# Starting the large arrays of a shared SBUF buffer on 64-byte lines

## The chip, the cores and the metric

The kernel runs on one core of a Trainium2 chip. The metric is the device time of one execution in microseconds, as the median of three runs.

## What is computed

The input `x` is four sequences of 1024 rows with 256 features. Four residual layers follow one another, each on the normalised rows:

```python
x = x + attn_a(layernorm(x))    # complex linear recurrence over time, dense layers, gelu, layernorm
x = x + ffn(layernorm(x))      # top-32 gating of outputs and inputs per row, 256x256 product
x = x + attn_b(layernorm(x))   # softmax attention, 8 heads of 64, keys and values through a rank of 64
x = x + ffn(layernorm(x))      # the same gated layer, same weights
```

The recurrence is an `associative_scan` with a complex factor per feature; its real and imaginary parts go through two 256x256 products, and two more dense layers follow. The gated layer takes a softmax of 256 logits per row, keeps the 32 largest (once to gate the outputs, once the inputs) and multiplies by one weight matrix:

```python
s_v_out, s_i_out = top_k(softmax(bottleneck_out(x)), 32)
out_branch = scatter(take(x @ weight, s_i_out) * s_v_out)
s_v_in, s_i_in = top_k(softmax(bottleneck_in(x)), 32)
in_branch = scatter(take(x, s_i_in) * s_v_in) @ weight
return out_branch + in_branch + bias
```

## The kernel before

The 4096 rows lie on 128 partitions as 32 tiles of 128 rows; eight chunks of four tiles make the units of the first layer. The program has four stages. The recurrence stage works chunk by chunk: TensorE projects the normalised rows (L1675, L1703), VectorE turns and scans them (L1334 to L1368), TensorE multiplies the states `h` (L1716) and the two dense layers (L1731 on `outT`, L1743 to L1749 on `y1T`). A gated layer works tile by tile: VectorE finds the 32 largest of 256 logits twice with eight MAX8 (L1487) and eight MATCH_REPLACE8 (L1492), ScalarE takes exponentials and moves PSUM results out (`zfT` at L983, `sxT` at L1028, `gs` at L1016, `fs` at L1023), GpSimd does seven elementwise steps of 128x256 (L743 to L762). The attention stage works through 64 items (batch, head, half of the rows); for each, TensorE computes the scores twice (L1966 with queries as weights for the row maxima, L1978 and L1980 with keys as weights) and the weighted sum (L1995 to L1997, 96 small matmuls with the exponentials `pr_hi` and `pr_lo` as weights and `lat` as the moving operand); ScalarE takes the exponentials (L1140) and rounds them to fp16 (L1148), and GpSimd and VectorE form the remainders (L819, L1592). The last stage is the gated layer again.

The order of the instructions on each engine is written out by hand; semaphores alone tie the engines together. Memory in SBUF is of two kinds. Some tensors are allocated by themselves (`x`, `zrow`, `zT`, `xcT`, `ident`, `fW`, `lin`, the transformed attention weights `qkA`, `voB` and others). Everything else is cut from one tensor, `arena`, of 27,800 four-byte words per partition, by a counter:

```python
        def carve(shape, dt=F32, parts=P):
            ...
            words = n if dt == F32 else (n + 1) // 2
            a = arena[0:parts, room[0]:room[0] + words]
            room[0] += words
```

The counter is set back to reuse the room in later stages: `room[0] = 0` before the gated layer's arrays, `room[0] = after_rows` before those of attention, `room[0] = after_setup` for the weights that are only transformed once. No array is padded, so a small array (`norm`, `obias`, `nm`, `sm` have two words each) shifts everything carved after it. In the built program `arena` itself begins at byte 96,992 of a partition, which is 32 bytes past a multiple of 64; of the separate tensors `x`, `xcT`, `ident`, `ident16` and `minus_ident16` begin on a multiple of 64, and `zrow`, `zT`, `fW`, `fbias`, `lin`, `qkA`, `voB` 32 bytes past one.

Of the kernel before, what the change touches and what calls it, by code (L numbers as in the profile page):

```python
# [37 lines left out]
GROUP = 4  # L38
GROUPS = NH // 2
Q_RING = 4  # L40
Z_RING = 4
AHEAD = 2

# [4 lines left out]
def hybrid_block_kernel(nc, x_in, W_in, b_in, params_log, W_mid, b_mid, w1_w, w1_b, w2_w, w2_b,  # L48
# [4 lines left out]
    with ctx:  # L53
# [51 lines left out]
        arena = sb("arena", [P, ARENA])  # L105
        room = [0]

        def carve(shape, dt=F32, parts=P):
            n = 1
            for s in shape:  # L110
                n *= s
            words = n if dt == F32 else (n + 1) // 2
            a = arena[0:parts, room[0]:room[0] + words]
            room[0] += words
            assert room[0] <= ARENA, room[0]
            if dt != F32:
                a = a.bitcast(dt)
            if len(shape) == 2:
                a = a.rearrange("p (a b) -> p a b", a=shape[0])
            if len(shape) == 3:  # L120
                a = a.rearrange("p (a b c) -> p a b c", a=shape[0], b=shape[1])
            return a


        cosT = carve([KB2, CH])
        win = carve([3, KB2, D])
        wmid = carve([2, KB2, D])
        w1 = carve([KB2, D])
        w2 = carve([KB2, D])
# [12 lines left out]
        gam = carve([D])  # L142
        sinT = carve([KB2, CH])
        decT = carve([KB2, CH])
        front_at = room[0]
        turned = [[carve([KB2, CH]) for _ in range(2)] for _ in range(2)]
        pa, pb = carve([KB2, CH]), carve([KB2, CH])
        ta, tb = carve([KB2, CH]), carve([KB2, CH])
# [15 lines left out]

        zf = [carve([D]) for _ in range(Z_RING)]
        zfT = [carve([KB2, P]) for _ in range(2)]
# [16 lines left out]
        after_ffn = room[0]  # L183
# [4 lines left out]
        pr_hi = [carve([TIME // P, CH], F16) for _ in range(2)]  # L188
        pr_lo = [carve([TIME // P, CH], F16) for _ in range(2)]

        room[0] = max(room[0], after_ffn)
        qA = carve([Q_RING, TIME], F16)
        qB_words = arena[:, room[0]:room[0] + Q_RING * TIME // 2]
        qB = carve([Q_RING, TIME], F16)
        kB_words = arena[:, room[0]:room[0] + TIME]
# [248 lines left out]
        def place(W):  # L444

            B, w = W // ITEMS, W % ITEMS
            hh, c = w // 2, w % 2
            return B, hh, c, hh % Q_RING

# [23 lines left out]
        def wait_from(engine, sem_, value):  # L473

            if value > 0:
                engine.wait_ge(sem_, value)
# [41 lines left out]
        def _(sp):  # L518
# [26 lines left out]
            def load(head):  # L545

                B, hh, slot = head // NH, head % NH, head % Q_RING
                if head % NH == 0:
                    for k in (2 * B, 2 * B + 1):
                        sp.wait_ge(s_qst[k], 2 * GROUPS * 16)  # L550
                wait_from(sp, s_qld, head * 48)
                wait_from(sp, a_sps, (head - Q_RING + 1) * 2 * KT)
                for half in range(2):
# [30 lines left out]
        def _(pool):  # L584
# [154 lines left out]
            def tail(f, t, p):  # L739
# [6 lines left out]
                pool.wait_ge(f_z, T + 1)  # L746
                nc.gpsimd.tensor_tensor(sx[p], dd[p][:, 1, :], zf[t % Z_RING], ALU.mult).then_inc(f_s, 1)
                pool.wait_ge(f_er, T * 2 + 2 + CREDIT["f_er"])
# [103 lines left out]
        def _(act):  # L852
# [118 lines left out]
            def z_tile(t, dst):  # L971
                return nc.scalar.activation(dst.unsqueeze(1), x[:, bass.ds(t, 1), :], ACT.Identity,
                                            bias=rs[:, bass.ds(t, 1), 1], scale=rs[:, bass.ds(t, 1), 0])

            def ffn_z(f, t):
                T = t + f * NT
                wait_from(act, f_s, T - Z_RING + 1)
                z_tile(t, zf[t % Z_RING]).then_inc(f_z, 1)

# [243 lines left out]
        def _(dve):  # L1223
# [413 lines left out]
            def last_tile(f, t, p):  # L1637
# [5 lines left out]
                dve.wait_ge(f_d_last, 1)  # L1643
                nc.vector.tensor_tensor(sx[p], dd[p][:, 1, :], zf[t % Z_RING], ALU.mult).then_inc(f_s, 1)
                dve.wait_ge(f_gps, T + 1)
# [10 lines left out]
        def _(pe):  # L1656
# [150 lines left out]
            def ffn_z_turned(f, t, p):  # L1807
                T = t + f * NT
                pe.wait_ge(f_z, T + 1)
                if not (isinstance(T, int) and T == 0):  # L1810
                    pe.wait_ge(f_zT, T + 0)
                z = zf[t % Z_RING]
                for k in range(KB2):
# [313 lines left out]
```

## Time and profile before

| | |
|---|---|
| median of three runs | 1379.68 us (1375.58 to 1380.49) |
| the profiled execution, its own time | 1381.49 us |
| its span in the trace | 1379.8 us |
| busy over the span | PE 88%, DVE 83%, ACT 76%, POOL 70% |
| mean granted TensorE clock | 0.968 of full speed |

"Busy" is the time in which an engine has an instruction in work. A matmul's duration in the trace includes its way through the array, so consecutive matmuls overlap; the distance from one start to the next tells their rate. The stages lie in the trace about at 0 to 260 us (recurrence), 260 to 505 us (first gated layer, with the projections of the first attention batches beside it), 505 to 1150 us (attention) and 1150 to 1380 us (second gated layer).

### The profile page before, as it was taken

What the parts mean: (1) busy time and instruction counts of PE and PEld (TensorE: products, weight loads), DVE (VectorE), ACT (ScalarE), POOL (GpSimd) and SP (SyncE); (2) the same over time, 40 slices, a digit from 0 to 9 for tenths busy, and PEclk for the clock granted to TensorE, in tenths of its full rate; (3) what the DMA queues carried; (4) which work ended last, traced back from release to release, by engine and by line L of the source; (5) the groups of instructions that cost most, each with busy time, mean ns of one, the idle gap of its engine ahead of it and who ended that gap; (6) DMA issues with size and microseconds to landing.
All of it is one profiled execution on the core that took longest, in us unless ns stands there. A gap on an engine that the chain in (4) does not pass through costs nothing.

```text
span 1379.8 us, 30641 instructions
## 1 busy us (share of the span) xinstructions
PE 1218.1 (88%) x10192; PEld 743.8 (54%) x10192; DVE 1149.0 (83%) x3141; ACT 1054.9 (76%) x2350; POOL 963.6 (70%) x1094
## 2 busy tenths in 40 slices
PE   3999999767888879999999999999999999667776
PEld 1455554334455536665666666666666666344444
DVE  6999998479998888888777787878777854799998
ACT  3432333677899869999999989999999985777775
POOL 4457644368777767778777778777777773488887
PEclk9999999989999999999999999999999999899997
DMA  6200000000012000000000000000000000000000
GB/s 174 77 1 1 0 1 0 1 1 1 12 36 77 31 17 25 25 25 25 25 13 14 2 2 2 2 3 2 2 2 2 2 2 1 1 31 17 31 17 31
DMA packets 35529, 25.32 MB, mean 18 GB/s; under 512 B 16358, under 2 KB 32044, under 8 KB 35372
## 3 DMA queue, kind: packets, MB, share of 16 engines
q1 hardware_dynamic: 35372, 23.36, 6.0%
q8 instruction: 82, 1.34, 0.4%
q14 instruction: 75, 0.61, 0.1%
HBM read 14.89 MB, written 8.39 MB: 17 GB/s over the span
## 4 chain that ended last, share of the span: by engine, by line
PE 57%; DVE 13%; issue 13%; ACT 12%; POOL 4%; DVEq 0%; DMA 0%; SPq 0%; ACTq 0%; POOLq 0%
PE banks L1978 7%; PE banks L1980 6%; PE banks L1966 6%; DVE arena L1492 4%; PE banks L1716 4%; PE banks L1924 4%; PE banks L1995 4%; PE banks L1996 4%; PE banks L1997 3%; DVE arena L1487 3%; ACT arena L1140 3%; PE banks L1675 3%; ACT arena L1148 2%; PE banks L1731 2%; PE banks L1900 2%
## 5 line engine op out<-in xcount | busy, mean ns | idle before, releaser
L819 POOL TENSOR_TENSOR arena<-arena 128x512 f16<-128x512 f32 x383 | 438.0, 1163 | 150.1 <-ACT arena L1148 146.4
L1140 ACT ACTIVATE arena<-banks 128x512 f32<-128x512 f32 x512 | 303.1, 600 | 45.1 <-PE banks L1980 40.3
L1566 DVE TENSOR_REDUCE arena<-banks 128x1 f32<-128x512 f32 x512 | 325.5, 679 | 5.1 <-PE banks L1966 2.8
L1148 ACT ACTIVATE arena<-arena 128x512 f16<-128x512 f32 x512 | 315.9, 632 | 0.0
L1487 DVE MAX8 arena<-arena 128x8 f32<-128x256 f32 x512 | 190.6, 414 | 27.4 <-issue 15.9
L1995 PE MATMUL banks<-arena 128*128 128x65 f16 x2016 | 211.3, 193 | 1.1
L1996 PE MATMUL banks<-arena 128*128 128x64 f16 x2016 | 211.4, 195 | 0.0
L1997 PE MATMUL banks<-arena 128*128 128x65 f16 x2016 | 210.5, 192 | 0.0
L1592 DVE TENSOR_TENSOR arena<-arena 128x512 f16<-128x512 f32 x129 | 106.8, 828 | 123.6 <-ACT arena L1148 123.5
L1492 DVE MATCH_REPLACE8 arena<-arena 128x256 f32<-128x256 f32 x512 | 206.0, 410 | 0.4 <-issue 0.2
L1995 PEld LDWEIGHTS banks<-arena 128*128 128x128 f16 x2016 | 187.9, 96 | 32.0 <-issue 10.1
L1996 PEld LDWEIGHTS banks<-arena 128*128 128x128 f16 x2016 | 187.3, 97 | 27.1
L1978 PE MATMUL banks<-arena 128*128 128x512 f16 x512 | 194.1, 379 | 8.2 <-ACT arena L1140 6.8
L1966 PE MATMUL banks<-arena 128*128 128x512 f16 x512 | 194.5, 382 | 4.6 <-DVE arena L1566 4.6
L1980 PE MATMUL banks<-arena 128*128 128x512 f16 x512 | 193.8, 378 | 0.0
L1997 PEld LDWEIGHTS banks<-arena 128*128 128x128 f16 x2016 | 187.4, 99 | 0.0
L1847 PE MATMUL banks<-fW,arena 128*128 128x256 f32 x256 | 80.5, 441 | 32.2 <-ACT arena L1028 32.2
L1966 PEld LDWEIGHTS banks<-arena 128*128 128x128 f16 x512 | 57.9, 113 | 74.5 <-DVE arena L1566 16.2
L1978 PEld LDWEIGHTS banks<-arena 128*128 128x128 f16 x512 | 50.3, 98 | 48.9 <-ACT arena L1140 31.5
L1834 PE MATMUL banks<-fW,arena 128*128 128x256 f32 x256 | 76.6, 428 | 0.0
L1826 PE MATMUL banks<-lin,xcT 128*128 128x512 f32 x128 | 71.5, 641 | 5.0 <-ACT xcT L1032 5.0
L1847 PEld LDWEIGHTS banks<-fW,arena 128*128 128x128 f32 x256 | 46.9, 203 | 52.1 <-ACT arena L1028 47.9
(223 smaller groups left out, 2543.3 us busy)
## 6 DMA issues: line engine op xcount, KB each, us to landing
arena<-q_store SPq DMA_DIRECT2D x48, 128.0 KB, 2.7
x<-in_L_attn_a_x SPq DMA_DIRECT2D x8, 512.0 KB, 3.9
q_store<-arena SPq DMA_DIRECT2D x32, 128.0 KB, 1.8
out<-x SPq DMA_DIRECT2D x7, 512.0 KB, 2.9
arena<-arena SPq DMA_DIRECT2D x64, 1.0 KB, 1.9
arena<-in_L_attn_a_W_in SPq DMA_DIRECT2D x1, 768.0 KB, 5.7
arena<-in_L_attn_a_W_mid SPq DMA_DIRECT2D x1, 512.0 KB, 7.5
arena<-in_L_attn_a_w_w SPq DMA_DIRECT2D x2, 256.0 KB, 7.8
```

What stands on the lines that cost most here:

```text
L819: nc.gpsimd.tensor_tensor(pr_lo[c][:, kt, :], pr[:, kt, :], pr_hi[c][:, kt, :], ALU.subtract).then_inc(a_lP, 1)
L1140: nc.scalar.activation(pr[:, kt, :], ps[6 + kt % 2][:, :], ACT.Exp, scale=SM_SCALE).then_inc(a_P, 1)
L1148: nc.scalar.activation(pr_hi[c][:, kt, :], pr[:, kt, :], ACT.Copy).then_inc(a_hi, 1)
L1487: nc.vector.max(m8[p][:, i, r, :], src).then_inc(f_k[i], 1)
L1492: nc.vector.match_replace(wk[p][:, i, r % 2, :], m8[p][:, i, r, :], src, TAKEN).then_inc(f_k[i], 1)
L1566: nc.vector.tensor_reduce(mx_half[c][:, i // 2, i % 2:i % 2 + 1], ps[n % MAX_BANKS][:, :], X, ALU.max).then_inc(a_mx, 1)
L1966: mm(ps[n % MAX_BANKS][:, :], every[:, j, :], kA[B % 2][:, half * CH:half * CH + CH], start=True, stop=True).then_inc(a_mps, 1)
L1978: mm(o[:, :], kA[B % 2][:, kt * P:kt * P + P], qA[:, slot, c * CH:c * CH + CH], start=True, stop=False)
L1980: mm(o[:, :], kB[B % 2][:, kt * P:kt * P + P], qB[:, slot, c * CH:c * CH + CH], start=False, stop=True).then_inc(a_sps, 1)
L1995: mm(o, pr_hi[c][:, kt, js], lat[B % 2][:, kt, 0:1 + HD], start=kt == 0, stop=False)
L1996: mm(o[:, 1:1 + HD], pr_hi[c][:, kt, js], lat[B % 2][:, kt, 1 + HD:], start=False, stop=False)
L1997: last = mm(o, pr_lo[c][:, kt, js], lat[B % 2][:, kt, 0:1 + HD], start=False, stop=kt == KT - 1)
```

## The change

`carve` moves the counter forward before every array of 16 words or more, to a position that is 8 modulo 16 words. Since `arena` begins 32 bytes (8 words) past a 64-byte line, such a position is the beginning of a 64-byte line. Arrays of less than 16 words are put wherever the counter stands. Two places that take a position from the counter themselves get the same rounding.

```diff
+LINE = 16
...
+        def on_line(at):
+
+            return at + (LINE // 2 - at) % LINE
+
         def carve(shape, dt=F32, parts=P):
             n = 1
             for s in shape:
                 n *= s
             words = n if dt == F32 else (n + 1) // 2
+            if words >= LINE:
+                room[0] = on_line(room[0])
             a = arena[0:parts, room[0]:room[0] + words]
...
-        front_at = room[0]
+        front_at = room[0] = on_line(room[0])
...
-        room[0] = max(room[0], after_ffn)
+        room[0] = on_line(max(room[0], after_ffn))
```

Every engine has the same instructions, in the same order, with the same shapes, waits and semaphore updates in both programs; only the element offsets of operands in `arena` differ. The bytes by which the arrays begin past a 64-byte line:

| arrays | before | after |
|---|---|---|
| `cosT`, `win`, `wmid`, `w1`, `w2`, `prm`; `z_rows[1]`, `zf`, `zfT`, `lg`, `wk`, `m8`; `pr`, `pr_hi`, `pr_lo`, `qA`, `qB`, `kA`, `kB`, `lat[0]` | 32 | 0 |
| `lng`, `lnb`, `gam`, `sinT`, `decT`, `turned`, `pa`, `pb`, `ta`, `tb`, `v`, `h`, `outT`, `outT2`, `y1T`, `yhat`, and the raw attention weights | 40 | 0 |
| `ex`, `exr`, `lat[1]` | 48 | 0 |
| `dd`, `sx`, `sxT`, `xb`, `fs`, `gs`, `ob`, `obx` | 16 | 0 |
| `o_sb[1]` (with `staged`), `oT` | 0 | 0 |

Only the beginnings are rounded. The rows of `lat` (129 fp16 each) are still 258 bytes apart, so that they begin 0, 2, 4 ... 14 bytes past the place of the first.

## Rows read from the trace of the kernel before

**Rows 1.** Windows: us; busy us (instructions) of each engine; clock; DMA share; GB/s.

```profile
0.00:260.00 260.00, 230.69 (x756) 122.43 (x756) 228.51 (x473) 96.44 (x189) 132.71 (x129) 0.98 0.12 34
260.00:505.00 245.00, 191.66 (x689) 107.03 (x690) 214.56 (x869) 195.14 (x517) 178.04 (x261) 0.94 0.08 25
505.00:1150.00 645.00, 628.47 (x8131) 414.22 (x8131) 499.13 (x961) 590.81 (x1184) 483.70 (x459) 1.00 0.04 9
1150.00:1380.00 230.00, 167.24 (x620) 100.16 (x618) 206.81 (x841) 172.50 (x462) 169.17 (x246) 0.90 0.06 19
```

**Rows 2.** The page: engines' shares of the chain that ended last.

```profile
PE 57%; DVE 13%; issue 13%; ACT 12%; POOL 4%; DVEq 0%; DMA 0%; SPq 0%; ACTq 0%; POOLq 0%
```

**Rows 3.** The chain in the recurrence stage: start us, us, what.

```profile
104.50 3.43 PE banks L1703 x8
107.93 0.87 PE banks L1662 x8
108.81 6.88 PE banks L1716 x16
115.69 3.43 PE banks L1675 x8
119.12 3.44 PE banks L1731 x8
```

**Rows 4.** The chain in attention, around 830 us: start us, us, what.

```profile
830.22 0.44 PE banks L1917 x4
```

**Rows 5.** Timeline of PE, attention's second batch: start us, duration us.

```profile
664.59 0.38 PE L1978 MATMUL banks<-arena 128*128 128x512 f16 x1
664.80 0.38 PE L1980 MATMUL banks<-arena 128*128 128x512 f16 x1
665.24 0.19 PE L1995 MATMUL banks<-arena 128*128 128x65 f16 x1
...
665.51 0.19 PE L1995 MATMUL banks<-arena 128*128 128x65 f16 x1
```

**Rows 6.** Timeline of PE, attention's third batch: start us, duration us.

```profile
832.53 0.19 PE L1995 MATMUL banks<-arena 128*128 128x65 f16 x1
...
832.80 0.19 PE L1995 MATMUL banks<-arena 128*128 128x65 f16 x1
```

**Rows 7.** Single lines of VectorE: count, then duration ns as min/median/max.

```profile
L1270 DVE BATCH_NORM_STATS2 nst<-x x96: 399/409/429, 104.0 to 1159.8; 128x6 f32<-128x256 f32 x96
...
L1487 DVE MAX8 arena<-arena x512: 401/412/429, 281.6 to 1370.3; 128x8 f32<-128x256 f32 x171
...
L1365 DVE TENSOR_TENSOR arena<-arena x8: 1209/1214/1220, 52.2 to 227.2; 128x1024 f32<-128x1024 f32 x8
```

**Rows 8.** Single lines of GpSimd: count, then duration ns as min/median/max.

```profile
L749 POOL TENSOR_TENSOR arena<-arena x63: 722/730/737, 292.3 to 1367.9; 128x256 f32<-128x256 f32 x63
...
L762 POOL TENSOR_TENSOR x<-arena x63: 723/729/738, 296.2 to 1371.2; 128x256 f32<-128x256 f32 x63
...
L819 POOL TENSOR_TENSOR arena<-arena x383: 1151/1160/1582, 507.4 to 1134.7; 128x512 f16<-128x512 f32 x192
...
L643 POOL TENSOR_TENSOR x<-x,arena x8: 1995/1997/2000, 99.8 to 262.6; 128x1024 f32<-128x1024 f32 x8
```

**Rows 9.** Groups of ScalarE: count, busy us, mean ns, idle time before.

```profile
L1140 ACT ACTIVATE arena<-banks 128x512 f32<-128x512 f32 x512 | 303.1, 600 | 45.1 <-PE banks L1980 40.3 <-POOL arena L819 2.9 <-issue 0.5
...
L1028 ACT ACTIVATE arena<-banks 128x256 f32<-128x256 f32 x64 | 24.5, 383 | 27.9 <-PE banks L1843 27.5
L983 ACT ACTIVATE arena<-banks 128x256 f32<-128x256 f32 x64 | 23.9, 374 | 11.2 <-PE banks L1814 10.9
...
L1126 ACT ACTIVATE arena<-banks 128x512 f32<-128x512 f32 x32 | 19.1, 599 | 15.6 <-PE banks L1917 15.6
```

**Rows 10.** DMA issues: count, KB each, median us from issue to landing.

```profile
x<-in_L_attn_a_x SPq DMA_DIRECT2D x8, 512.0 KB, 3.9
...
arena<-in_L_attn_a_W_in SPq DMA_DIRECT2D x1, 768.0 KB, 5.7
```

## The prediction

> **What bounds the kernel now.** I read the windows by stage first. In attention TensorE is busy 628.47 of 645 us at full clock, so that stage lasts as long as its matmuls do. In the recurrence stage TensorE is busy 230.69 of 260 us and VectorE 228.51. In the second gated layer VectorE leads with 206.81 of 230 us, and in the stretch of the first one with 214.56 of 245, with TensorE and ScalarE close behind [rows 1]. The chain that ended last says the same: PE 57%, DVE 13%, ACT 12%, POOL 4%, and DMA 0% [rows 2]. The reader is to see that there is no idle resource whose release could give time, and that transfers decide nothing after the start. Whatever this change gives or costs must come out of the duration of single instructions, above all TensorE's, for the instruction lists are the same. So the whole question is whether an instruction's duration depends on where in a 64-byte line its operand begins. The kernel before answers most of it by itself, because its operands begin at 0, 16, 32, 40 and 48 bytes past a line. I compare like with like, engine by engine.
>
> **TensorE in attention.** Its operands move from 32 to 0. The 512-column fp16 score matmuls start 0.21 to 0.22 us apart (664.59 and 664.80) [rows 5]; at full clock, 2.4 GHz, 512 columns are 0.213 us at one a cycle, so there is nothing more than some 2 ns to gain in one. The weighted sums read `lat[1]`, 48 past a line, in the second batch and `lat[0]`, 32 past, in the third. Nine matmuls take 665.51 - 665.24 = 0.27 us in one and 832.80 - 832.53 = 0.27 us in the other, 30 ns each [rows 5, 6]. A 65-column matmul needs 27 ns at one column a cycle. That leaves 3 ns which could have to do with the weights, since `pr_hi` and `pr_lo` begin 32 past a line in both. Against that stand the fp32 transposes of 128 columns: their moving operand `ident` begins at 0 in all, and their weights are `zrow` at 32 (L1662) or `o_sb[1]` at 0 (L1917). Eight take 0.87 us and four 0.44 us, 109 and 110 ns each [rows 3, 4]. So weights at 0 are read no faster than weights at 32. As to moving operands, that at 0 (`ident`, 109 ns for 128 columns) and that at 32 (`zT` of L1703, 3.43 / 8 = 429 ns for 512) stand as 1 to 3.93; with a fixed part f and a part per column the two give f = 109 - 107 = 2 ns, which is again the small remainder at 0 as at 32. Value taken for attention: 0.
>
> **TensorE in the recurrence stage.** Here there is a difference to see. L1703 and L1675 stream `zT`, which begins at 32 and doesn't move: 3.43 us for 8, 428.8 ns each. L1716 streams `h` and L1731 `outT`, both at 40: 6.88 us for 16 and 3.44 us for 8, 430.0 ns each [rows 3]. After the change both begin at 0. If they then stream as `zT` does, each gains 1.25 ns. There are 16 of L1716 and 8 of L1731 in each of the 8 chunks, 192 in all: 192 x 1.25 = 0.2 us, all on the path. By rounding of the rows to 0.01 us the difference is between 0.3 and 1.9 ns, so 0.1 to 0.4 us. Value taken: 0.2 us.
>
> Which arrays differ at all can also be asked of the Trainium skill. "SBUF — State Buffer", section "Specifications (TRN2)", puts SBUF's lines at 16 bytes, each crossing to a new line being paid for; of the offsets here only 40 is off a 16-byte line. By that rule the arrays of the recurrence stage would gain and none of the others, which the trace bears out for `h` and `outT`; the sum would be the same 0.2 us, and the next paragraph's 0.6 us would be nothing.
>
> **ScalarE.** Writing `oT`, which begins at 0, takes 599 ns for 128x512 out of PSUM; writing `pr` at 32 takes 600 [rows 9]. So L1140 gains nothing. Of two copies of the same form, 128x256 out of PSUM, the one into `zfT` at 32 takes 374 ns and that into `sxT` at 16 takes 383 (L983, L1028) [rows 9]. They also read different PSUM banks, and I take the 9 ns as that: 0. If it is the offset, the 64 of L1028, for which L1847 waits, give 64 x 9 = 0.6 us. That is the bound on the side of a gain; with 599 against 600 there is none on the side of a loss.
>
> **VectorE.** MAX8 over 256 logits at 32 takes 412 ns, and the statistics of 256 elements of `x` at 0 take 409 (L1487, L1270) [rows 7]. The 128x1024 add of the recurrence stage, all operands at 40, takes 1214 (L1365) [rows 7]. From 256 to 1024 elements that is (1214 - 409) / 768 = 1.05 ns an element, and the same slope from 0 would leave 409 - 268 = 141 ns for both. Offset 40 with two inputs costs nothing beside offset 0 with one. Value taken: 0. The 3 ns between MAX8 and the statistics is the bound: 512 MAX8 and as many MATCH_REPLACE8, all in the two stages that VectorE leads, 1024 x 3 = 3.1 us.
>
> **GpSimd.** `x` at 0 from `gs` and `obx`, both at 16, takes 729 ns (L762); `sx` at 16 from `dd` at 16 and `zf` at 32 takes 730 (L749); 512 elements at 32 take 1160 (L819); 1024 elements of `x` at 0 and `yhat` at 40 take 1997 (L643) [rows 8]. From 256 to 512 elements the slope is (1160 - 730) / 256 = 1.68 ns, from 256 to 1024 it is (1997 - 730) / 768 = 1.65. A straight line through four offsets. Value taken: 0, with 1 ns for each of the 7 x 63 = 441 small steps of the two gated layers as the bound to either side, 0.4 us.
>
> **DMA.** `x` begins at 0 and takes 3.9 us for 512 KB, `W_in` goes to 32 and takes 5.7 us for 768 KB [rows 10]: 7.6 and 7.4 ns a KB. The offset makes no difference, and DMA's share of the chain is 0% [rows 2]. The 1 KB copies of the row maxima into `qB` go to another offset too, but their pieces are 8 bytes each, before and after. Value taken: 0.
>
> **Sum.** The profiled execution took 1381.49 us, 1.7 more than its span; 1381.49 - 0.2 = 1381.3. It lies 1.8 us above the median of the runs, 1379.68, and so the prediction for the median is 1379.68 - 0.2 = 1379.5 us. The bounds add up to 0.4 + 0.6 + 3.1 + 0.4 = 4.5 us less and 0.4 us more: 1375.2 to 1380.1. The three runs of before spread from 4.1 below to 0.8 above their median, and a median of new runs will do so too. A measurement of this kernel can tell a difference of about 0.5%, 6.9 us, from none.
>
> **Rivals.** *Lines of 64 bytes are what the engines read by, and a start at 0 saves a step where one at 32 doesn't show it.* The 2 to 3 ns over a column a cycle in each matmul speak for it. Against it: the same remainder with `ident` at 0 [rows 3, 4]. Priced with the 1.25 ns that `h` shows, over attention's 1536 + 6048 = 7584 matmuls on the path, it would give 9.5 us: 1370.2. Chance 0.09.
>
> *Operands that now begin at the same place of a line hinder one another.* This is the case on the other side. Before, TensorE's moving `lat[1]` (48) and its weights (32) differed in place in every second batch, and two of `x`'s partners (`lnb`, `yhat` at 40) differed from `x` in the recurrence stage; after, all of them are at 0. Its place is attention's weighted sum. It is slower by more than 0.5% from 6.9 / 6.048 = 1.1 ns a matmul on; at 1.25 ns on all 7584 the time would be 1389.2. Against it: `lat[0]` and the weights are both at 32 in the third batch, and the rate is the same 30 ns [rows 6]; L762 with both inputs at 16 is no slower than L749 with 16 and 32 [rows 8]. Chance 0.05.
>
> *The granted clock falls at other moments.* It was 0.90 and 0.94 in the two gated layers and 0.98 in the recurrence stage [rows 1]. At half rate, 1.2 GHz instead of 2.4, a stretch of matmuls takes twice its time. In the last stage a clock of 0.90 over 230 us is 2 x 0.10 x 230 = 46 us at the lower level, of which VectorE hides nearly all. A shift would be worth a few us of either sign; 7 us need 14 us more at the lower level where TensorE is the bound. Nothing in the change drives it. Chance 0.04, half on each side.
>
> *The change doesn't do what it says* has little room: the arrays do begin on lines. But the rows within `lat` go on beginning 0 to 14 bytes past one, and small arrays anywhere, so what depends on those stays as it was. That falls together with the forecast.
>
> **How the numbers follow.** The forecast, no effect but 0.2 us with bounds of -4.5 and +0.4 us, has 0.82. With the rival of 64-byte lines at 0.09 and half the clock's 0.04, faster by over 0.5% has 0.11; with the collision at 0.05 and the clock's other half, slower has 0.07. The range takes the bounds of the forecast together with the runs' spread: 1375.2 less a good part of 4.1 gives 1372.5, and 1380.1 with 0.8 and some for a lower clock 1384.5.
>
> **What would show it.** Right: L1716 x16 in the chain at 6.86 us instead of 6.88, L1028 still 383 ns, MAX8 412, L819 1160, nine weighted matmuls still 0.27 us, and attention as long as before. It is wrong if the distance between two weighted matmuls falls under 29 ns or rises over 31, if L819's and L1592's medians move by over 1%, or if L1140 moves by over 5 ns: each would mean that an offset which the trace before doesn't contain for that operand, 0, has a price of its own.

## The result, and the profile after

The changed kernel takes 1383.91 us (median of nine runs, 1382.21 to 1387.32); the kernel before, run between them on the same chip, 1380.49 us (nine runs). The ratio over these runs is 1.0036, with a 95% interval from 1.0024 to 1.0048; the two medians alone lie 0.25% apart. That is inside the 0.5% which the prediction called no change, and inside its range, but it isn't nothing: the interval lies wholly above 1, and the forecast was 0.2 us less, not 3.4 us more. The profiled execution took 1383.85 us, with a span of 1382.0 us and a mean granted clock of 0.967 (0.968 before), so the clock isn't the reason.

First the windows by stage of the changed kernel, with the columns of [rows 1].

```profile
0.00:260.00 260.00, 229.49 (x734) 120.88 (x735) 229.75 (x462) 93.62 (x184) 141.56 (x127) 0.97 0.12 34
260.00:505.00 245.00, 191.89 (x703) 108.94 (x701) 213.80 (x874) 197.13 (x521) 178.39 (x261) 0.93 0.07 25
505.00:1150.00 645.00, 627.71 (x8120) 412.12 (x8121) 502.55 (x966) 590.02 (x1183) 483.86 (x460) 1.00 0.04 9
1150.00:1380.00 230.00, 167.86 (x638) 101.65 (x636) 207.24 (x842) 172.58 (x464) 168.89 (x246) 0.92 0.06 19
```

Against [rows 1] one busy time stands out: GpSimd, the last engine of each row, had 132.71 us of work in the recurrence stage and has 141.56. Everywhere else it has the same to within 0.4 us. The landmarks of the two traces agree; all times here count from the start of the span, as in the rows. VectorE's last addition of the recurrence stage (L1368 before, L1375 after; all lines of `kernel.py` stand 7 further on in the changed kernel) starts at 228.3 us before and at 232.6 after, 4.3 us late. The first MAX8 is 3.7 us late, attention's first exponential 3.8, its last 3.5. From the start of the first of these exponentials to that of the last it is 628.8 us before and 628.5 after; from the first MAX8 of the last stage to the last one 188.8 and 188.6. So the loss arises before 233 us and is only carried on after that.

Now GpSimd's long steps, single lines with count and duration as min/median/max in ns. The first three rows are of the changed kernel (L619, L628 and L643 of before).

```profile
L626 POOL TENSOR_TENSOR arena<-arena x16: 2347/2358/3337, 43.7 to 225.1; 128x1024 f32<-128x1024 f32 x16
L635 POOL TENSOR_TENSOR x<-x,arena x8: 2354/2365/3373, 55.3 to 211.5; 128x1024 f32<-128x1024 f32 x8
L650 POOL TENSOR_TENSOR x<-x,arena x8: 2349/2362/2373, 101.6 to 267.2; 128x1024 f32<-128x1024 f32 x8
```

The same view of the kernel before, for two of these lines; the third, L643 with 1997 ns, stands in [rows 8].

```profile
L619 POOL TENSOR_TENSOR arena<-arena x16: 1997/2364/3339, 43.3 to 220.5; 128x1024 f32<-128x1024 f32 x16
L628 POOL TENSOR_TENSOR x<-x,arena x8: 1995/2002/3004, 54.6 to 207.1; 128x1024 f32<-128x1024 f32 x8
```

The additions to `x` went from 1997 and 2002 ns to 2362 and 2365. L619 multiplies `v[0]` once by `cosT` and once by `sinT`. Its row of before had a minimum of 1997 and a median of 2364: the products with `cosT` were fast (seven of eight at 1997 to 2003 ns) and those with `sinT` slow (2362 ns or more) already. That row would have told of the effect before the change was run; the prediction didn't use it.

A stretch of the sixth chunk shows how this reaches the other engines. Timelines of GpSimd and VectorE, start us and duration us; the kernel before, one row of each engine:

```profile
157.21 2.00 POOL L628 TENSOR_TENSOR x<-x,arena 128x1024 f32<-128x1024 f32 x1
...
158.52 1.77 DVE L1342 TENSOR_TENSOR arena<-arena 128x1024 f32<-128x1024 f32 x1 [0.22 <-DVE conv L1424]
```

And the changed kernel:

```profile
160.54 2.35 POOL L635 TENSOR_TENSOR x<-x,arena 128x1024 f32<-128x1024 f32 x1
...
161.86 2.12 DVE L1349 TENSOR_TENSOR arena<-arena 128x1024 f32<-128x1024 f32 x1 [0.22 <-DVE conv L1431]
```

VectorE's addition of two SBUF operands takes 1.2 us when nothing is in its way (1225 to 1227 ns in the seven other chunks of before). Here it begins 1.3 us after GpSimd's step in both kernels and takes 1.77 us in one and 2.12 in the other: GpSimd's 0.35 us come back as VectorE's 0.35 us. "SBUF — State Buffer" in the Trainium skill, section "Who interferes with whom", says that a VectorE instruction with two SBUF inputs contends with a GpSimd instruction that reads SBUF; the trace agrees. A second VectorE line shows it too. Single lines of VectorE, L1343 of before, and the same line, L1350, of the changed kernel:

```profile
L1343 DVE TENSOR_TENSOR arena<-arena x8: 1211/1220/3022, 39.8 to 213.4; 128x1024 f32<-128x1024 f32 x8
```

```profile
L1350 DVE TENSOR_TENSOR arena<-arena x8: 1212/1218/3387, 40.1 to 217.7; 128x1024 f32<-128x1024 f32 x8
```

The median is unchanged at 1.22 us, and the longest grew by 365 ns. In the experiments below it follows GpSimd's additions to `x`: 3019 to 3025 ns where they are fast, 3384 to 3385 where they are slow.

Last the chain that ended last. The page of the changed kernel, engines' shares:

```profile
PE 53%; DVE 16%; issue 14%; ACT 13%; POOL 4%; DVEq 0%; DMA 0%; SPq 0%; ACTq 0%; POOLq 0%
```

And pieces of its chain in the recurrence stage: start us, us, what.

```profile
124.67 1.00 issue
...
134.20 1.23 DVE arena L1349
135.50 3.15 issue
138.66 2.33 DVE arena L1358 x2
...
144.31 1.22 DVE arena L1358
```

Two rows of the timelines of GpSimd and VectorE at the same place, start us and duration us:

```profile
134.27 3.37 POOL L635 TENSOR_TENSOR x<-x,arena 128x1024 f32<-128x1024 f32 x1
...
135.35 3.38 DVE L1350 TENSOR_TENSOR arena<-arena 128x1024 f32<-128x1024 f32 x1
```

TensorE went from 57% to 53% and VectorE from 13% to 16% [rows 2]. Where the chain before lay on TensorE without a break, [rows 3] and on to 145 us, it now lies on VectorE's turns and scans. The two engines were close in this stage, 230.69 and 228.51 us of 260 [rows 1], and 0.36 us on each long GpSimd step was enough to put VectorE in front. GpSimd itself hardly appears: 4% before and after. Its cost is booked on VectorE. The 3.15 us called "issue" at 135.50 lie inside L1350, which starts at 135.35 and lasts 3.38 us because it runs beside GpSimd's L635: that is the long duration of the row above, and no engine is named for it.

### The profile page after: what moved, and what is told of

Read it like the earlier page. It is cut to its first block, busy times and chain, and to the rows that moved or that the text cites. A ratio compares the mean times of both kernels' runs of the same rounds, so it can differ in the third digit from the quotient of the medians.

```text
span 1382.0 us, 30641 instructions
## 1 busy us (share of the span) xinstructions
PE 1217.0 (88%) x10192; PEld 743.6 (54%) x10192; DVE 1153.3 (83%) x3141; ACT 1053.3 (76%) x2350; POOL 972.7 (70%) x1094
## 4 chain that ended last, share of the span: by engine, by line
PE 53%; DVE 16%; issue 14%; ACT 13%; POOL 4%; DVEq 0%; DMA 0%; SPq 0%; ACTq 0%; POOLq 0%
PE banks L1985 7%; PE banks L1987 6%; PE banks L1973 6%; DVE arena L1499 4%; PE banks L1931 4%; PE banks L2002 4%; PE banks L2003 4%; PE banks L2004 3%; ACT arena L1147 3%; DVE arena L1494 3%; PE banks L1723 2%; PE banks L1682 2%; ACT arena L1155 2%; PE banks L1907 2%; ACT arena L1009 1%
## 5 line engine op out<-in xcount | busy, mean ns | idle before, releaser
L826 POOL TENSOR_TENSOR arena<-arena 128x512 f16<-128x512 f32 x383 | 437.5, 1162 | 150.4 <-ACT arena L1155 146.6
L2004 PE MATMUL banks<-arena 128*128 128x65 f16 x2016 | 210.4, 192 | 0.0
```

Source lines behind the costliest of these rows:

```text
L826: nc.gpsimd.tensor_tensor(pr_lo[c][:, kt, :], pr[:, kt, :], pr_hi[c][:, kt, :], ALU.subtract).then_inc(a_lP, 1)
L2004: last = mm(o, pr_lo[c][:, kt, js], lat[B % 2][:, kt, 0:1 + HD], start=False, stop=kt == KT - 1)
```

## The experiments

**The disputed cost by itself.** A kernel in which GpSimd alone multiplies two arrays, with start places and lengths varied, four times each:

```python
nc.gpsimd.tensor_tensor(A[:, OUT + po:OUT + po + n], A[:, p0:p0 + n], A[:, 4096 + p1:4096 + p1 + n], ALU.mult)
```

> Leaves out the whole computation (the output is a copy of x): it measures two-input elementwise steps of GpSimd with every other engine idle, then some of VectorE alone. First input at the start of a 64-byte line or some words past it, second input 4096 words and some words further, output 8192 words further, four times each. Theory A (GpSimd is slow where both inputs begin at the same place of a line): 1024 elements take about 2360 ns for the same place (0 and 0, 2 and 2, 8 and 8) and about 2000 ns for 2, 4, 6, 8, 10, 12, 14 words apart, wherever the output is; 256 elements 729 in both, as in the two traces; VectorE 1214 in all. Rival B (what counts is whether an operand begins on a line): 0 and 0, 0 and 2, 0 and 8 all take 2360, 2 and 2 takes 2000. Rival C (the 365 ns are VectorE's reads that collide with GpSimd's): all take 2000, for VectorE is idle.

Its timeline, start us and us for four instructions. The pairs of start places, in words of 4 bytes, are in order (0,0), (0,1), (0,2), (0,4), (0,8), then both inputs and the output at 2; then 256 elements at (0,0) and (0,2), and 512 elements into fp16 at (0,0) and (0,2).

```profile
14.56 9.59 POOL L41 TENSOR_TENSOR A<-A 128x1024 f32<-128x1024 f32 x4
24.23 8.23 POOL L44 TENSOR_TENSOR A<-A 128x1024 f32<-128x1024 f32 x4
32.54 8.21 POOL L47 TENSOR_TENSOR A<-A 128x1024 f32<-128x1024 f32 x4
40.83 9.59 POOL L50 TENSOR_TENSOR A<-A 128x1024 f32<-128x1024 f32 x4
...
58.80 9.59 POOL L56 TENSOR_TENSOR A<-A 128x1024 f32<-128x1024 f32 x4
...
94.73 9.60 POOL L68 TENSOR_TENSOR A<-A 128x1024 f32<-128x1024 f32 x4
...
184.48 3.12 POOL L101 TENSOR_TENSOR A<-A 128x256 f32<-128x256 f32 x4
187.69 2.78 POOL L104 TENSOR_TENSOR A<-A 128x256 f32<-128x256 f32 x4
...
282.98 4.84 POOL L143 TENSOR_TENSOR A<-A 128x512 f16<-128x512 f32 x4
287.90 4.85 POOL L146 TENSOR_TENSOR A<-A 128x512 f16<-128x512 f32 x4
```

Median durations, ns, of all cases:

| case | ns |
|---|---|
| 1024 elements, inputs 0, 4, 8, 12, 16 or 32 words apart | 2338 to 2339 |
| 1024 elements, inputs 1, 2, 6, 10 or 14 words apart | 1995 to 1998 |
| 1024 elements, inputs both at 1, 2, 4 or 8; output at 0, 2 or 8 | 2338 to 2342 |
| 1024 elements in place, inputs 0 and 10 words apart | 2338 and 1995 |
| 128; 256; 512; 768; 2048 elements, same place against 2 words apart | 454, 408; 722, 636; 1261, 1089; 1801, 1542; 4494, 3808 |
| 512 elements, fp32 less fp16 into fp16, 0, 2, 4, 8 or 12 words apart | 1152 to 1154 |
| VectorE, 1024 elements, 0, 2 or 8 words apart | 1225 |

What counts is neither the line nor a place on it but the difference of the two inputs' starts: a multiple of 16 bytes is slow, every other distance that was tried (1, 2, 6, 10 and 14 words) fast. The cost goes with the length: 86 ns at 256, 343 at 1024, 686 at 2048 elements, a third of a ns per element. The output's place is indifferent, and so is everything in the mixed fp16 case and on VectorE. The expectation that 256 elements wouldn't depend on it was wrong.

**One half of the change each.** Only the arrays of the recurrence stage on lines, and only all the others:

```diff
+        rounded = [True]
...
-            if words >= LINE:
+            if words >= LINE and rounded[0]:
...
         room[0] = 0
+        rounded[0] = False
...
-        room[0] = on_line(max(room[0], after_ffn))
+        room[0] = max(room[0], after_ffn)
...
+        rounded[0] = True
```

(the second kernel has `False` and `True` exchanged, keeps the last rounding and leaves out that of `front_at`).

> Only the recurrence stage's arrays (and the raw attention weights carved behind them) are rounded to lines; those of the gated layers and of attention stay where they were. Theory A: all of the loss is in GpSimd's 25 long steps of this stage, so as slow as the changed kernel, ratio to before 1.002 to 1.005, 128x1024 steps at 2360 ns. Rival D (the loss comes from the arrays of the other stages as well): ratio nearer to 1.000, under 1.002.

> The other half: only the arrays of the gated layers and of attention are rounded to lines, the recurrence stage keeps its offsets. Theory A: no difference from before, ratio 0.999 to 1.001, and L619, L628, L643 as before at 1997 (half of L619 at 2362). Rival D: slower than before by 0.2% or more.

The first took 1384.36 us, ratio 1.0026 (1.0013 to 1.0038), with the additions to `x` at 2362 and 2363 ns; the second 1379.87 us, ratio 0.9998 (0.9983 to 1.0012), at 1998 and 1995. The whole loss goes with the recurrence stage's arrays. Rounding those of attention and of the gated layers gives nothing that can be measured. The second has its last addition of the stage at 228.3 us as the kernel before, the first at 234.2, which is 1.6 us later than the changed kernel with the same GpSimd durations. In that execution the granted clock was 0.57 from 50 to 54 us, where the changed kernel had 1.00, and the 1.6 us are there from the second chunk on; whether the clock made them was not tried.

**Off the common place again.** The changed kernel, with a few arrays two words past their line, so that no two inputs of a long GpSimd step are a multiple of 16 bytes apart. That frees the second half of L619 too, which was slow before the change.

```diff
-                room[0] = on_line(room[0])
+                room[0] = on_line(room[0]) + skew
...
-        lnb = carve([D])
-        gam = carve([D])
+        lnb = carve([D], skew=2)
+        gam = carve([D], skew=2)
...
-        v = [carve([KB2, CH]) for _ in range(2)]
+        v = [carve([KB2, CH], skew=2 * (1 - i)) for i in range(2)]
...
-        yhat = carve([TPC, D])
+        yhat = carve([TPC, D], skew=2)
```

> The changed kernel, with four arrays put 8 bytes past the line: lnb, gam, yhat and the first of v, so that in each long GpSimd step of the recurrence stage the two inputs begin at different places. Theory A: all 33 steps of 1024 elements take 2000 ns, the 8 that took 2360 before too; the stage gets back the 3.7 us that the change cost and may gain some 2 to 3 us more by the 8 steps, so 1376 to 1380 us against 1380.5, ratio 0.997 to 1.000. Rival B (an operand on a line is the slow thing): x and g's partners still begin on lines, so as slow as the changed kernel, 1.002 or more.

1380.21 us, ratio 0.9993 (0.9978 to 1.0007): the loss is gone. Single lines of this kernel:

```profile
L626 POOL TENSOR_TENSOR arena<-arena x16: 1995/2000/2981, 43.3 to 219.6; 128x1024 f32<-128x1024 f32 x16
L650 POOL TENSOR_TENSOR x<-x,arena x8: 1993/1997/2000, 99.4 to 264.1; 128x1024 f32<-128x1024 f32 x8
L1350 DVE TENSOR_TENSOR arena<-arena x8: 1212/1218/3021, 39.8 to 212.6; 128x1024 f32<-128x1024 f32 x8
```

VectorE's last addition of the stage starts at 227.1 us, 5.5 before the changed kernel and 1.2 before the original one. The longest of VectorE's L1350 is back at 3021 ns.

**No line at all.** The kernel before, with one array of two words ahead of `lng`. None of the recurrence stage's large arrays in `arena` begins on a 64-byte line then; those that stood at 40 stand at 48.

```diff
+        pad = carve([2])
```

> The kernel before with one unused array of two words carved ahead of lng: everything of the recurrence stage behind it moves from 40 to 48 bytes past a line, nothing begins on a 64-byte line that didn't before. Theory A, as the probe narrowed it (GpSimd's step is slow where its two fp32 inputs begin a multiple of 16 bytes apart): lnb, gam, yhat, v are now 16-byte multiples from x, win, cosT and sinT, so all 33 steps of 1024 elements take 2340 to 2370 ns and the kernel is as slow as the changed one, ratio 1.002 to 1.005. Rival B (it takes a start on a 64-byte line): as before, 1.000.

1383.12 us, ratio 1.0021 (1.0008 to 1.0034). Single lines:

```profile
L620 POOL TENSOR_TENSOR arena<-arena x16: 2347/2361/3335, 43.7 to 225.1; 128x1024 f32<-128x1024 f32 x16
L629 POOL TENSOR_TENSOR x<-x,arena x8: 2357/2364/3363, 55.3 to 211.5; 128x1024 f32<-128x1024 f32 x8
L644 POOL TENSOR_TENSOR x<-x,arena x8: 2347/2363/2368, 101.6 to 264.5; 128x1024 f32<-128x1024 f32 x8
```

They start and last as in the changed kernel, and VectorE's last addition starts at 232.6 us in both. Eight bytes of padding reproduce the change, without a single line of 64. This is the run that takes the 64-byte line out of the explanation of the loss.

**Which steps.** The changed kernel with only `lnb`, `gam` and `yhat` two words off (the additions to `x` and the scaling of the weights fast), and with only `v[0]` off (both products fast):

```diff
-        lnb = carve([D])
-        gam = carve([D])
+        lnb = carve([D], skew=2)
+        gam = carve([D], skew=2)
...
-        yhat = carve([TPC, D])
+        yhat = carve([TPC, D], skew=2)
```

```diff
-        v = [carve([KB2, CH]) for _ in range(2)]
+        v = [carve([KB2, CH], skew=2 * (1 - i)) for i in range(2)]
```

> The changed kernel with lnb, gam and yhat alone put 8 bytes past the line: the 17 steps on x and win fast (2000 ns), the 16 products with cosT and sinT slow (2360). Theory A: the residual add L643 feeds the next statistics and frees yhat; if the loss comes through it, the stage ends as early as before and the ratio is 1.000; if it comes through the products, on which VectorE waits, the ratio stays at 1.002 to 1.004. I expect most of it from the products: 1.002.

> The changed kernel with v[0] alone put 8 bytes past the line: the 16 products with cosT and sinT fast, the 17 steps on x and win slow. The other half of e5: if the products carry the loss, ratio 0.999 to 1.001; if the steps on x do, 1.002 to 1.004. I expect 1.001.

1381.51 us, ratio 1.0006 (0.9993 to 1.0018), and 1381.93 us, 1.0007 (0.9990 to 1.0023). The medians don't tell the two apart. The landmarks do better: VectorE's last addition starts at 230.4 us where the products are slow and at 228.9 where the additions to `x` are, against 227.1 with all fast and 232.6 with all slow. So the 16 products cost 3.3 us and the 16 additions 1.8, and both together 5.5. These are single profiled executions, but kernels whose long GpSimd steps are slow in the same places have this landmark at the same time: 228.3, 228.3 and 228.4 us in three of them, 227.1 in three, 232.6 in two. The one exception is the 234.2 us above. Part of what the products cost can be seen: VectorE's own product L1366 runs beside them in the third, fourth and fifth chunks and takes 1.7 us there where they are slow, against 1.2 to 1.3 where they are fast, 1.3 us over the stage. The rest of the 3.3 us is not placed.

**The gated layers, slow all along.** Their seven GpSimd steps had inputs a multiple of 16 bytes apart in both kernels. The first of these three kernels adds to the skewed one above two words for `exr`, `dd`, `xb`, `obx` and `fbias`; the second does the like in the kernel before and leaves its recurrence stage alone; the third is the second with pads in the recurrence stage too, ahead of `sinT`, `v[0]`, `v[1]` and `yhat`, and nothing rounded to lines. The longer `fbias` moves `arena` itself 32 bytes on in all three, onto a 64-byte line. So in the first of them the rounded arrays begin 32 bytes past a line and none of them on one, and in the other two the arrays that stood at 32 (`cosT`, `win`, `zf`, `lg`, `pr` and others) begin on a line without having been rounded.

```diff
-        fbias = sb("fbias", [P, D])
+        fbias = sb("fbias", [P, D + 8])[:, 2:2 + D]
...
-        exr = [carve([2, D]) for _ in range(2)]
+        exr = [carve([2, D], skew=2) for _ in range(2)]
...
-        dd = [carve([2, D]) for _ in range(2)]
+        dd = [carve([2, D], skew=2) for _ in range(2)]
...
-        xb = [carve([D]) for _ in range(2)]
+        xb = [carve([D], skew=2) for _ in range(2)]
...
-        obx = [carve([D]) for _ in range(2)]
+        obx = [carve([D], skew=2) for _ in range(2)]
```

> The skewed kernel e3, and in the gated layers exr, dd, xb, obx and fbias put 8 bytes further too, so that each of the seven 128x256 steps of GpSimd has its inputs 8 bytes apart modulo 16. (By the longer fbias the arena itself begins 32 bytes further, which keeps every 16-byte place.) Theory A: the seven steps take about 640 ns in place of 727, 0.6 us less GpSimd work per tile and 38 us of busy time over 63 tiles. VectorE leads there, so I expect little of it in the time: 0.996 to 0.9995 of before. Theory that 128x256 steps don't depend on the place, as my prediction read the trace: 727 ns and ratio 0.9993 as e3.

> The kernel before with unused pairs of words carved between the gated layers' arrays, and a longer fbias, so that each of GpSimd's seven 128x256 steps a tile has its two inputs 8 bytes apart modulo 16; the recurrence stage and attention keep their 16-byte places. Theory A: the seven steps at 640 ns in place of 729, the 1024-element steps as before (25 at 1997, 8 at 2362). If the gain of e7 over before (0.28%) comes from the gated layers, the ratio is 0.997 to 0.999; if it came from the recurrence stage, 1.000. I expect 0.998.

> e8 and the same in the recurrence stage, by pads ahead of sinT, v and yhat: every GpSimd step with two fp32 inputs has them 8 bytes apart modulo 16, as in e7, but no array is rounded to a line and most begin 16 to 56 bytes past one. Theory A (the 16-byte places alone count): as e7, ratio 0.996 to 0.999, the last state of the recurrence (L1368) about 239.5 us into the trace as in e3 and e7. If starts on 64-byte lines gave something of their own, e7's 0.9972 would not be reached.

| kernel | median us | ratio, interval | recurrence stage's last VectorE addition starts |
|---|---|---|---|
| all apart, rounded arrays 32 past a line | 1376.92 | 0.9972 (0.9957 to 0.9987) | 227.1 us |
| gated layers alone, not rounded | 1377.29 | 0.9986 (0.9971 to 1.0001) | 228.4 us |
| all apart, not rounded | 1377.36 | 0.9988 (0.9971 to 1.0006) | 227.1 us |

Each ratio is to the kernel before in runs beside it, whose median was 1380.14 us for the first and 1379.13 for the other two. The expectation's 239.5 us is the end of the same addition, counted from the beginning of the record, which lies some 11 us ahead of the span's start.

Groups of GpSimd in the first of them, count, busy us, mean ns, idle time before:

```profile
L750 POOL TENSOR_TENSOR arena<-arena 128x256 f32<-128x256 f32 x63 | 40.3, 639 | 43.5 <-ACT arena L1016 43.3
L762 POOL TENSOR_TENSOR arena<-arena 128x256 f32<-128x256 f32 x63 | 40.3, 639 | 49.7 <-ACT arena L1030 49.7
```

The seven steps went from 729 to 639 ns, 441 x 90 ns = 39.7 us of GpSimd's work; the windows of the two gated layers show 38.8 less than [rows 1]. Most of it turned into idle time: in the changed kernel the second of these lines waited 32.0 us in all, here 49.7. From the first MAX8 of the first gated layer to the last it is 210.4 us before, 209.3 in the first of these kernels and 208.0 in the other two; in the last stage it is 188.8 before and 188.6 to 188.7 in all three. There VectorE leads by [rows 1], and GpSimd is ahead of it. The first of the three beats the kernel before by 0.3% and has the lowest median of all; the changed kernel was not run beside it. The other two have intervals that contain 1. All three overlap one another, so they don't tell whether a start on a line is worth anything by itself. Nothing here says that it is: the one version clearly faster than the kernel before has no rounded array on a line.

## Why the prediction was wrong

**What bounds the kernel: right, and applied too narrowly.** That all had to come from the durations of single instructions was right, and so was that TensorE and VectorE were close in the recurrence stage. The clause "above all TensorE's" drew the eye to the wrong engine.

**TensorE, ScalarE and VectorE: right; DMA right in the time.** L1716 and L1731 were to gain 1.25 ns each. The chain of the changed kernel has these lines, seven further on, as:

```profile
191.13 6.87 PE banks L1723 x16
...
201.43 3.43 PE banks L1738 x8
```

6.87 and 3.43 stand where [rows 3] has 6.88 and 3.44; over all starts the mean distance of L1716 is 430.4 ns before and 429.3 after. The 0.2 us are real, and lost in the rest. But the gain isn't one of 64-byte lines. The mean is 430.4 ns in the three kernels whose `h` begins at 40 or at 8, and 429.3 in the eight where it begins at 0, 32 or 48, the one with the two-word pad (48) among them. The unit is 16 bytes, as in the rule that the prediction set beside its sum. (Two slips of its arithmetic change nothing: by its own rounding the difference lies between 0.3 and 2.2 ns, not 1.9; and 6048 weighted matmuls are those that the trace holds, while 64 items of 96 make 6144, so that rival's price is 9.6 us.) As groups, with count, busy us, mean ns and idle time before:

```profile
L1147 ACT ACTIVATE arena<-banks 128x512 f32<-128x512 f32 x512 | 302.8, 599 | 45.2 <-PE banks L1987 40.3
...
L1035 ACT ACTIVATE arena<-banks 128x256 f32<-128x256 f32 x64 | 24.5, 382 | 27.4 <-PE banks L1850 27.1
...
L1494 DVE MAX8 arena<-arena 128x8 f32<-128x256 f32 x512 | 190.4, 413 | 26.9 <-issue 15.4
...
L826 POOL TENSOR_TENSOR arena<-arena 128x512 f16<-128x512 f32 x383 | 437.5, 1162 | 150.4 <-ACT arena L1155 146.6
```

ScalarE's 599 and 382 answer to 600 and 383 [rows 9]; the 9 ns between `sxT` and `zfT` stay with both at 0, so they weren't the offset. MAX8's mean of 413 answers to 414 before (medians 411 and 412 [rows 7]), the fp16 remainder's 1162 to 1163 (medians 1159 and 1160 [rows 8]). The weighted matmuls start 30.6 ns apart in both. `W_in` landed in 5.3 us, against 5.7 [rows 10], with no DMA in the chain. That the offset makes no difference to a DMA doesn't hold for this transfer: it landed in 5.3 to 5.5 us in the seven traces where it begins on a 64-byte line and in 5.7 to 5.9 in the four where it begins 32 bytes past one. The transfers behind it show no such split (`W_mid` 7.0 to 7.5 us in both cases), and nothing of it reaches the time. The bounds of 0.6 us for L1028 and 3.1 us for VectorE weren't called on.

**GpSimd: the step that failed.** The prediction said: "A straight line through four offsets. Value taken: 0", with 0.4 us as the bound. The term should have been 25 long steps of the recurrence stage that grow by 0.36 us each, about 9 us of GpSimd's work, on a path that VectorE shares. The line went through steps of different kinds. The 256-element steps, 729 and 730 ns, had inputs a multiple of 16 bytes apart and were slow. The 512-element one reads fp32 and fp16 and writes fp16, a form that doesn't depend on the places. The 1024-element one, with `x` at 0 and `yhat` at 40, was fast. Like with like, from the kernel with GpSimd alone, the two lines are 722 and 2338 ns, or 636 and 1995. The prediction's comparison of `x` at 0 with its partner at 40 was the only one of the three that the change altered, and it had no partner in the slow case to stand beside. L619 would have been one: two products of the same form and length, one with `cosT` at 32, one with `sinT` at 40, `v[0]` at 40 in both. The place of one operand was looked at where a pair of them mattered.

What it was worth: 25 steps, 24 in the chunks (one product and two additions in each of eight) and the scaling of the weights, by 0.36 us make 9.0 us of GpSimd's work, and the window shows 8.85. About half, 4.3 us, came out of the stage; 3.5 us of it are left at attention's last exponential and 2.2 in the two spans, and the medians differ by 3.4.

**The rival of the collision: the mechanism was near, the place and the size weren't.** It had a chance of 0.05. "Operands that now begin at the same place of a line hinder one another" names the thing, and `lnb` and `yhat` as `x`'s partners were in it. It was placed on TensorE's weighted sum, where nothing moved. The evidence raised against it, L762 no slower than L749, compared two steps that were both slow: 16 and 16 bytes, and 16 and 32 (the step whose operands are these is L747, at 727 ns; L749 has both at 48), are both multiples of 16. The line of 64 bytes was the wrong unit.

**Lines of 64 bytes as a gain, and the clock.** Attention gained nothing (628.8 and 628.5 us), and the clock gave 0.967 for 0.968. The sentence on what would make the prediction wrong listed L819 and L1592, L1140 and the weighted sum, all of which held; the lines that moved weren't among them. That the time still fell inside the range is luck: the range was made of the runs' spread and of bounds for other terms, and only 0.4 us of it stood for a slower GpSimd.

**What stays open.** What in GpSimd's reading gives the 16 bytes their part was not tried. Distances of 3 words modulo 4 and other operations than add, subtract and multiply were not tried either. Nor is it settled where the 3.2 us of the fastest version come from within the stages. Its recurrence stage is 1.2 us shorter and its first gated layer about 1, in one execution, and the first MAX8 moves by some 2 us between executions (281.6 us before, 279.8 in the kernel with the same recurrence stage and the rest on lines).

## What to carry to other kernels

Compare a pair of operands with a pair, and only steps of one form: three durations on a straight line prove little when length, type and places all differ between them. A line whose minimum and median lie far apart (1997 and 2364 ns here) holds two cases, and is the first place to look before anything is moved. For GpSimd's fp32 steps with two inputs, keep the distance of the inputs' starts off a multiple of 16 bytes, two words of padding being enough; and expect a step off the path to cost through the engine that shares its reads. When a start is rounded relative to a buffer, look again where the buffer itself begins after every edit: a longer `fbias` was enough to take all the rounded arrays off their lines.

## What the runs showed of the hardware

A GpSimd elementwise step with two fp32 inputs in SBUF takes 2338 ns for 1024 elements if the inputs' starts differ by a multiple of 16 bytes and 1995 to 1998 at the other distances tried (4494 and 3808 for 2048). "GPSIMD Engine Reference" in the Trainium skill, section "Elementwise — side-by-side cycle accounting", gives one figure for an add, 4497 ns for 2048, and calls the two reads sharing a port the floor. The slow case agrees with the figure, and the fast one lies 15% under it. A step from fp32 and fp16 into fp16 (512 elements) takes 1152 to 1154 ns wherever the inputs begin, and VectorE's 1225 ns for 1024 don't depend on it either. TensorE's fp32 matmuls of 512 columns start 430.4 ns apart if the moving operand begins 8 or 40 bytes past a 64-byte line and 429.3 if it begins 0, 32 or 48 past one; its fp16 matmuls, whose operands went from 32 to 0, start 30.6 ns apart before and after. One DMA of 768 KB into SBUF landed in 5.3 to 5.5 us on a 64-byte line and in 5.7 to 5.9 us 32 bytes past one; others beside it showed no difference.
